# Layer norm's products and its low half on VectorE instead of GpSimd, and two key scalings at other steps

## What is computed

```python
def attn_layer(x, Wqkv, qs, ksc, Wo):            # 16 heads of 64, window 32
    q, k, v = split(x @ Wqkv, 3)
    q, k = l2norm(q) * qs, l2norm(k) * ksc
    q, k = rotary(q) * scale, rotary(k) / scale
    return local_attention(q, k, v) @ Wo
def ffn_layer(x, g, bln, W1, b1, W2, b2):
    mu = x.mean(-1, keepdims=True)
    var = ((x - mu) ** 2).mean(-1, keepdims=True)
    xn = (x - mu) / jnp.sqrt(var + 1e-05) * g + bln
    a, gate = split(xn @ W1 + b1, 2)
    return a * gelu(gate) @ W2 + b2
for i in range(6):
    x = attn_layer(shift_tokens(x), ...) + x
    x = ffn_layer(shift_tokens(x), ...) + x
```

## Time and profile before

| | |
|---|---|
| median of 3 runs | 3610.63 us (3610.14 to 3611.5) |
| the profiled execution | 3610.49 us |
| its span in the trace | 3608.7 us |
| busy share of PE / DVE / ACT / POOL | 91% / 84% / 83% / 80% |

### The profile page before, as it was taken

One profiled execution on the slowest core, in us unless ns is written; L12 is line 12 of the kernel. 1 busy time (PEld: TensorE's weight loads), 2 busy tenths in 40 slices (PEclk: granted clock), 3 DMA queues, 4 the chain that ended last, 5 costly groups with the idle time before them and its releaser, 6 DMA issues.

```text
span 3608.7 us, 92500 instructions
## 1 busy us (share of the span) xinstructions
PE 3292.0 (91%) x29710; PEld 2114.4 (59%) x29710; DVE 3038.7 (84%) x10488; ACT 3011.2 (83%) x8812; POOL 2879.2 (80%) x2383
## 2 busy tenths in 40 slices
PE   7887899999999999999999999999999999999998
PEld 3444566656666556666656666656666666666665
DVE  7997888888888888888888888888888888888886
ACT  6554888888888888888888888888888888888887
POOL 6787887887887887887888887888887887887883
PEclk9999999999999999999999999999999999999999
DMA  5443323333323333322333322333322333332322
GB/s 167 136 133 123 110 101 103 105 115 105 115 102 103 104 113 104 115 101 102 107 114 106 116 102 100 108 116 103 116 103 98 108 115 105 115 104 98 107 101 92
DMA packets 261726, 396.22 MB, mean 110 GB/s; under 512 B 45566, under 2 KB 86588, under 8 KB 261244
## 3 DMA queue, kind: packets, MB, share of 16 engines
q1 hardware_dynamic: 261244, 390.30, 32.2%
HBM read 157.91 MB, written 6.03 MB: 45 GB/s over the span
## 4 chain that ended last, share of the span: by engine, by line
PE 47%; ACT 30%; DVE 13%; issue 7%; POOL 2%; DMA 0%; DVEq 0%; ACTq 0%; SPq 0%; POOLq 0%
ACT pr L1182 13%; PE bank L884 9%; PE bank L873 7%; PE bank L844 5%; PE bank L360 4%; PE bank L362 4%; PE bank L912 4%; PE bank L361 4%; ACT sq L1170 4%; DVE ab L1608 3%; DVE wide L1500 3%; PE bank L854 3%; PE bank L829 2%; DVE sm L1656 2%; PE bank L855 2%
## 5 line engine op out<-in xcount | busy, mean ns | idle before, releaser
L1182 ACT ACTIVATE pr<-sm,nb,rq 128x128 f32<-128x128 f32 (+1 forms) x3072 | 1518.3, 501 | 159.2 <-DVE nb L1667 158.3
L1343 POOL TENSOR_TENSOR pr<-pr,rden 128x640 f32<-128x640 f32 x768 | 964.9, 1256 | 492.5 <-DVE rden L1633 488.5
L1357 POOL TENSOR_TENSOR rot<-ab,swp 128x512 f32<-128x512 f32 x760 | 977.2, 1286 | 78.9 <-DMA swp<-ab 78.2
L1608 DVE TENSOR_TENSOR ab<-bank,ltab 128x1024 f32<-128x1024 f32 x760 | 925.4, 1218 | 92.1 <-PE bank L362 83.4
L1656 DVE CUSTOM_DVE_ANT_0 sm<-bank,mask 128x128 f32<-128x128 f32 (+1 forms) x3072 | 766.0, 302 | 119.4 <-ACT pr L1182 113.3
L1182 ACT ACTIVATION_READ_ACCUMULATOR pr<-sm,nb,rq 128x1 f32 x3072 | 597.3, 194 | 0.0
L1170 ACT ACTIVATE sq<-bank 128x512 f32<-128x512 f32 x768 | 453.9, 591 | 101.2 <-DVE ab L1608 95.0
L1643 DVE COPY pt<-bank 128x512 f32<-128x512 f32 x768 | 529.5, 689 | 9.9 <-PE bank L855 2.8
L854 PE MATMUL bank<-ident,pr 128*128 128x128 f32 x1536 | 397.9, 286 | 142.7 <-DVE pt L1643 142.5
L1363 POOL TENSOR_TENSOR rot<-rot,rkb 128x512 f32<-128x512 f32 x384 | 493.2, 1290 | 21.4 <-DMA rkb<-k_scratch 21.0
L873 PE MATMUL bank<-pt,vtok 128*64 128x160 f32 (+1 forms) x6144 | 461.1, 292 | 52.2 <-ACT vtok L1196 52.2
(11 more groups left out here) (213 smaller groups left out, 5700.4 us busy)
## 6 DMA issues: line engine op xcount, KB each, us to landing
swp<-ab SPq DMA_DIRECT2D x1520, 128.0 KB, 2.1
rkb<-k_scratch SPq DMA_DIRECT2D x768, 128.0 KB, 2.9
rot<-c_scratch SPq DMA_DIRECT2D x64, 256.0 KB, 3.3
sq<-c_scratch SPq DMA_DIRECT2D x64, 256.0 KB, 3.2
xs<-xT SPq DMA_DIRECT2D x95, 128.0 KB, 2.3
xs<-xT SPq DMA_DIRECT2D x95, 127.5 KB, 2.4
raw<-Wqkv SPq DMA_DIRECT2D x48, 128.0 KB, 2.6
wo<-Wo SPq DMA_DIRECT2D x6, 512.0 KB, 4.5
```

The lines of the kernel that those rows point to most:

```text
L1182: ins = act.activation(pr[:, s % 4, i, t, 0:P + WINDOW * t], sm[:, s % 2, i, cs], ACT.Exp, bias=nb[:, s, t, i:i + 1], scale=head_scale(rq, ...
L1343: ins = pool.tensor_tensor(pr[:, e % 4, :, :, :], pr[:, e % 4, :, :, :], rden[:, e, :, :].rearrange("p t i -> p i t").unsqueeze(3) .to_bro ...
L1357: pool.tensor_tensor(rot[:, PAIRS * (j % 2) + j // 2, :], ab_of(j, 0, lead), swp_of(j, lead), ALU.add).then_inc(qk_rot, 1)
L1608: dve.tensor_tensor(ab_both(j, lead).rearrange("p i (b t) -> p i b t", b=GB), seqs(qk_bank(j, lead)[:, :]).unsqueeze(1).to_broadcast(shape ...
```

## The change

`normed` and `low` go from GpSimd to VectorE. `normed` becomes one instruction, xn = (xn * g) * xv, without the addition of b. ScalarE adds b when it rounds: `xn_h` is now Identity with a bias read from `lv` in place of Copy. `low` becomes (xn + b) - xn_h, one instruction as before. The semaphore f_xn goes, and so does GpSimd's wait for the layer's vectors (lv_ok). In the tables, `scale_k` of pair 1 moves from step 14 of the turn before to step 0 of the turn that uses it, that of pair 3 from step 2 to step 4, and `spread_k_norm` of pair 5 from step 4 to step 5.

```diff
@@ SPREAD_STEPS, SCALE_STEPS
- 4: ('cur', 5)}
+ 5: ('cur', 5)}
 SCALE_STEPS = {13: [('cur', 7)],
+ 0: [('cur', 1)],
  1: [('cur', 2)],
+ 4: [('cur', 3)],
+ 5: [('cur', 4)],
  7: [('cur', 5)],
  9: [('cur', 6)],
- 14: [('next', 0), ('next', 1)],
- 2: [('cur', 3)],
- 5: [('cur', 4)]}
+ 14: [('next', 0)]}
@@ ScalarE
                         act.wait_ge(f_gb, n1 + (prev + 1))
-                        act.activation(xn_h[:, :], xn, ACT.Copy).then_inc(f_hi, 1)
+                        act.activation(xn_h[:, :], xn, ACT.Identity, bias=lv[:, V_B:V_B + 1]).then_inc(f_hi, 1)
@@ GpSimd
-                def normed(q):
-                    ready = (n1 + (q + 1))
-                    vectors = (l + 2) if kind == "T2" else None
-                    if vectors is not None:
-                        pool.wait_ge(lv_ok, vectors)
-                    pool.wait_ge(f_xc, ready)
-                    pool.wait_ge(f_rstd, ready)
-                    pool.tensor_tensor(xn, xn, xv, ALU.mult).then_inc(f_xn, 1)
-                    pool.wait_ge(f_xn, ready)
-                    pool.tensor_scalar(xn, xn, lv[:, V_G:V_G + 1], lv[:, V_B:V_B + 1], ALU.mult, ALU.add)\
-                        .then_inc(f_gb, 1)
-
...
-                def low(q):
-                    pool.wait_ge(f_hi, n1 + (q + 1))
-                    pool.tensor_tensor(xn_l[:, :], xn, xn_h[:, :].bitcast(F32), ALU.subtract).then_inc(f_split, 1)
...
-                    if prev is not None and kind != "drain":
-                        if s == AT["norm"]:
-                            normed(prev)
-                        if s == AT["low"]:
-                            low(prev)
@@ VectorE
+                def normed(q):
+                    dve.wait_ge(f_xc, n1 + (q + 1))
+                    dve.wait_ge(f_rstd, n1 + (q + 1))
+                    dve.scalar_tensor_tensor(xn, xn, lv[:, V_G:V_G + 1], xv, ALU.mult, ALU.mult).then_inc(f_gb, 1)
+
+                def low(q):
+                    dve.wait_ge(f_hi, n1 + (q + 1))
+                    dve.scalar_tensor_tensor(xn_l[:, :], xn, lv[:, V_B:V_B + 1], xn_h[:, :].bitcast(F32),
+                                             ALU.add, ALU.subtract).then_inc(f_split, 1)
...
+                    if s == AT["norm"] and prev is not None and kind != "drain":
+                        normed(prev)
+                    if s == AT["low"] and prev is not None and kind != "drain":
+                        low(prev)
```

## The result

| | median | range | ratio to before (95%) |
|---|---|---|---|
| before | 3610.39 us (4 runs) | 3607.97 to 3611.5 | |
| changed kernel | 3650.26 us (4 runs) | 3645.8 to 3655.18 | 1.0112 (1.0094 to 1.0129) |

The account below looks back on a forecast made before the run. The prediction took the chain through ScalarE and VectorE, then TensorE alone, as the bound. Its terms, 46 x (0.74 + 0.05 + 0.03) = 37.7 us on 3610.5, gave 3647 us, about 1% slower, range 3620 to 3675.

Parts of the forecast that it names:

- What bounds: Whole turn: ScalarE and VectorE alternate on the chain, then TensorE alone; GpSimd, busy 80%, holds only 2% of it.
- `low`, 0.74 us a turn: Step 11: VectorE waits for `xn_h`, 1.83 us later; step 12 takes back 1.09, and 0.74 reaches the square of block 12.
- The reserve of step 12: VectorE, step 12: the 0.37 us wait for ScalarE, 0.08 of overlap and 0.64 from the held `nb`, 1.09 us.
- `normed`, 0.05 us a turn: Step 10 on VectorE: nearly all fits in the wait for the exponentials; 0.05 us a turn, ends 0 and 0.31.
- GpSimd's relief, 0: Over 2.6 us of work leaves GpSimd in every turn, but it is off the chain: gain 0.
- The reserve of 1.79: VectorE, step 10: its wait of 1.79 us for ScalarE's exponentials, into which `normed` was to fit.
- long rows of `normed`: Sign of a wrong forecast: rows of `low` or `normed` on VectorE that are long and end with a GpSimd row.
- The tables, 0.03 us a turn: Moved scalings cost 0; pair 5's late fetch makes GpSimd 0.9 to 1.4 us later: 0.03 a turn, ends 0 and 0.3.
- The holds: Rival: both new VectorE instructions wait out a GpSimd instruction and `nb` stays held; 3680 likelier, 137 us at most; chance 0.10.
- No difference: Rival: TensorE truly bounds the second stretch, so the 0.74 sinks into its waits; 3604 to 3617; chance 0.07.
- Hidden in part: Rival: VectorE has more reserve in step 12 than seen; 0.2 to 0.5 a turn, 3620 to 3633; chance 0.07.
- Faster: Rival: GpSimd's hold on VectorE was the real cost; ScalarE gains 0.32 us a turn in step 12, 3596; chance 0.04.

Follow-up runs that it names:

- after: The changed kernel itself, with the whole change, against the kernel before: 3650.26 us, ratio 1.0112.
- e9: The changed kernel with `xn_h` one copy later on ScalarE, behind the copy of values of step 11: 3675.63 us, 1.0186 to before.
- e10: The kernel before without GpSimd's two products of `normed`, left out of the computation, `low` still on GpSimd: 3606.44 us, 0.9983 to before.
- e8: e5 with 1/sqrt(var) written to PSUM, so that `normed` reads only one large input in SBUF: 3605.48 us, 0.9983 to before.
- e11: e7 with 1/sqrt(var) written to PSUM, where `normed` reads it: 3589.33 us, 0.9942 to before.
- e1: The changed kernel with the old tables, so the layer norm half of the change alone: 3640.67 us, 1.008 to before.
- e3: The changed kernel with the norm fetch for pair 5 put back from step 5 to step 4: 3638.53 us, 1.0075 to before.
- e12: The changed kernel with `low` at step 12 on VectorE and all the tables as before: 3588.63 us, 0.9935 to before.
- e7: The changed kernel with `low` at step 12 on VectorE and the fetch for pair 5 back at step 4: 3586.96 us, 0.9938 to before.
- e6: The changed kernel with `low` at step 12, behind the products of block 11, on VectorE: 3603.87 us, 0.998 to before.
- e5: The changed kernel with `xn_h` ahead of the square of block 10 and pair 5's fetch back at step 4: 3604.63 us, 0.9979 to before.

## Why the prediction was right, and where its terms were off

**What bounds.** The chain of the earlier trace rows, from steps 10 to 12 on ScalarE and VectorE and then on TensorE alone, was the right thing to read. No stretch behind square 12 gives the lost time back: +0.0 us in after, and a later `xn_h` in e9 ended 25 us later. The reading that GpSimd's 80% says little held nearly as well: without `normed`'s two products on it, 97 us of work, the kernel is 6 us faster (e10).

**`low`, 0.74 us a turn.** Every part of this term can be seen. The forecast said an idle time of some 1.1 us released by `xn_h`; it is 1.08 in the turn shown and 51.1 / 47 = 1.09 in the mean. `xn_h` was to be 0.10 longer, and is 0.09 (712 for 623 ns). The pointer to the bias changed, and with it Copy became Identity. The Trainium skill, ScalarE: Activation LUTs, "What ACT_TABLE_LOAD costs", has about 93 ns for each pointer operand; the trace, with 89, agrees. No hold at `low` was expected, and there is none. The reserve of step 12 was to give the wait of 0.37 and the hold of `nb`, 0.64: both are gone from the rows. The square of block 11 was to be 0.8 us late, and is 0.83 in the median turn. The loss carried to square 12 is 0.73 in the typical turn, against 0.74. The sum, 46 x 0.74 = 34 us, is 4 too many: in the 5 turns that split new weights, the square of block 11 is only 0.31 us late, and in 6 others VectorE had more reserve, so that square 12 is 0.37 late. One turn doesn't stand quite for all. The measured sum is 29.6.

**`normed`, 0.05 us a turn, and GpSimd's relief, 0.** 2.3 us forecast for both. The reserve of 1.79 went down to 0.42 in the median turn and was used up in 3 of 46. The hold that I took into account is frequent (median 1149 against 750 ns), and nearly always covered. The forecast had named long rows of `normed` as a sign of being wrong; they came, and cost nothing (e8, e11). What the stretch from square 8 to square 10 shows without the late fetch is a gain, 3.2 us in e1 and 3.5 in e3, which is GpSimd's relief (e10: 3.7). So the two terms together were 5 to 6 us too high.

**The tables, 0.03 us a turn.** This step failed. The place was named (the fetch of pair 5 behind the loads of `xs`, then `nb` of the entries behind it), but the size wasn't: 1.4 us forecast, 12 by e3 and 11.8 by the stretches. Two numbers were wrong. I let GpSimd come 0.9 to 1.4 us later; it came 1.93 later in the median turn and up to 2.96. The 2.9 us that I took to landing is the median of single DMAs, but a fetch is two, issued 0.6 us apart, and from the first issue to the last landing it takes 3.84 us in the median and up to 4.91. And I put the effect at `nb` of entry 10 and its weight near the lower end of 0 to 0.3 a turn, where it was 0.26. It meets the `nb` of entries 8 and 9 and the products of block 8 instead. The other moves are worth nothing, as forecast (e12 against e7).

**The sum came out by luck in part.** Forecast were 34 for `low`, 2.3 for `normed` and 1.4 for the tables, together 37.7. The stretches have 29.6 for `low`, -3.5 for `normed` and the relief, and 11.8 for the fetch, together 37.9. Errors of -4, -6 and +10 us cancel, and the forecast of 3647 lies nearer to 3650 than its parts deserve. There are some 3 us more outside of all this (`after` begins its first turn 1 us later, and takes 2 us longer behind the last square of block 12), which I can't explain.

**The rivals.** "The holds", 3680, was wrong at its own condition: GpSimd was idle when `low` came. "No difference" was wrong since nothing behind gives time back. "Hidden in part" asked for more reserve in step 12; 6 turns of 46 had it. "Faster", 3596, was wrong for this kernel for the reason given there: with `xn_h` behind the square, ScalarE can't start it before VectorE's products. But its mechanism is real. Once `low` costs no wait, the freed `nb` is worth about what was worked out, 46 x 0.32 = 15 us: in e6 and e7 the stretch from exponentials 12 to square 12 is 17.9 and 17.7 us shorter than before.

**The chain's GpSimd share.** I had written nothing on it. It isn't a price. With 2% (e1, e3) the kernel takes 3639 to 3641 us, and e5, in which GpSimd has 22%, takes 3605. e5's page:

```profile
PE 28%; POOL 22%; issue 16%; DVE 16%; ACT 14%; DMA 4%; SPq 1%; DVEq 0%; POOLq 0%; ACTq 0%
```

On a kernel whose engines meet every microsecond, the chain that ended last can go over another engine in long stretches without that engine being what costs.

## What to carry to other kernels

An instruction moved to an engine that executes in order costs what it waits for, and all that stands behind it pays; its own length comes second. Here the same two instructions made the kernel 1.1% slower (1.0112, 1.0094 to 1.0129) with `low` in front of its input, and 0.6% faster (0.9938, 0.9924 to 0.9952) with `low` one step later and the fetch in its old place, so put such an instruction where the timeline shows its input made, and look at what stands between on the engine that makes it. If a transfer is moved back in its queue, count from its first issue to its last landing, and compare the time to its reader with the longest of these and not with the median of one DMA.

## What the runs showed of the hardware that was not expected

- **The hold between VectorE and GpSimd goes both ways, and one operand in PSUM ends it.** VectorE's 128x512 `normed` with two large inputs in SBUF took 750 to 1895 ns in after; 37 of the 47 took over 800, and each of these ended 546 to 554 ns after the end of a GpSimd instruction. With one of the inputs in PSUM it took 746 to 749 (e8). GpSimd's rotation, 1.28 us in the median and never over 1.34 in the kernel before, takes up to 1.77 in after; the 37 over 1.34 all lie beside `normed`. GpSimd in after, beside `normed` of 1811.95:

```profile
1812.10 1.74 POOL L1358 TENSOR_TENSOR rot<-ab,swp 128x512 f32<-128x512 f32 x1
```

  and in e7, beside `low` of 1791.83:

```profile
1792.16 1.56 POOL L1358 TENSOR_TENSOR rot<-ab,swp 128x512 f32<-128x512 f32 x1 [0.74 <-DMA swp<-ab]
```

  In both, VectorE had begun first (1811.95 against 1812.10, 1791.83 against 1792.16), and the rotation is 1.74 - 1.28 = 0.46 us longer in the one and 0.28 in the other. The Trainium skill, SBUF — State Buffer, "Who interferes with whom", says that the order of issue decides who blocks whom, and that a VectorE instruction with at most one SBUF input, outside its two-port modes, isn't concerned. The trace agrees with both: the later one is the one that gets longer, and with one input in PSUM `normed` never does.
- **The hold falls hardest, for their length, on the smallest instructions.** Of the 768 products `nb` of 128x4 in the kernel before, 249 took over 250 ns, and every one of these ended within 24 ns of the end of a GpSimd instruction. Together the 768 took 273 us (mean 355 ns), where at the 0.16 us of a free one they would take 123. The mean is 291 in after and 269 in e7.
- **The landing of a small fetch varies by 1.5 to 1.8 us from turn to turn at one place.** From the first issue of pair 5's fetch to its last landing it took 3.34 to 5.10 us in the kernel before, and 3.44 to 4.91 in after, behind the two loads of `xs`. The median rises from 3.49 to 3.84 us. Whether these loads or other traffic of that step raise it wasn't tested.
